# The first self attention's weighing: exponentials as the stationary operand, outputs by tokens

## The reference

```python
qkv = jnp.einsum('bsh,hf->bsf', x, W_qkv)          # 256 tokens x 1536
q8, q_scale = act_quant(q)                          # likewise k8, v8
scores = jnp.einsum('bhqd,bhkd->bhqk', q8, k8) * (q_scale * k_scale) / sqrt(32)
attn = jax.nn.softmax(scores, axis=-1)
out = jnp.einsum('bhqk,bhkd->bhqd', attn, v8) * v_scale
out = out.transpose(0, 2, 1, 3).reshape(B, S, H)
return jnp.einsum('bso,oh->bsh', out, W_out) + b_out   # the caller adds x
```

## Time and profile before

| | us |
|---|---|
| median of 3 runs | 1639.95 (1639.75 to 1640.92) |
| the profiled execution: time | 1641.43 |
| the profiled execution: span | 1639.6 |
| busy in the span: TensorE, its operand loads | 1611.7 (98%), 1250.7 (76%) |
| busy in the span: VectorE, ScalarE, GpSimd | 1086.7 (66%), 690.1 (42%), 131.0 (8%) |

### The profile page before, as it was taken

One profiled execution on the slowest core, in us unless ns is written; L12 is line 12 of the kernel. 1 busy time (PEld: TensorE's weight loads), 2 busy tenths in 40 slices (PEclk: granted clock), 3 DMA queues, 4 the chain that ended last, 5 costly groups with the idle time before them and its releaser, 6 DMA issues.

```text
span 1639.6 us, 22511 instructions
## 1 busy us (share of the span) xinstructions
PE 1611.7 (98%) x8732; PEld 1250.7 (76%) x8732; DVE 1086.7 (66%) x1733; ACT 690.1 (42%) x933; POOL 131.0 (8%) x218
## 2 busy tenths in 40 slices
PE   9999999999999999999999999999999999999998
PEld 7887888888888888888888888887757746555454
DVE  4445777777778778777777779999583741743333
ACT  4334454444445454444454446555331321322221
POOL 0001000000100000010000001111100000011110
PEclk9999999999999999999999999999999999999999
DMA  7876655554565556555454454334320517479994
GB/s 237 226 227 189 161 132 154 149 151 122 170 163 142 148 142 154 119 184 142 119 138 124 128 135 123 102 92 150 121 112 18 205 52 287 197 233 427 422 423 183
DMA packets 125513, 282.93 MB, mean 173 GB/s; under 512 B 7712, under 2 KB 83680, under 8 KB 119264
## 3 DMA queue, kind: packets, MB, share of 16 engines
q1 hardware_dynamic: 103104, 200.75, 38.8%
q0 software_dynamic: 22304, 80.75, 16.5%
HBM read 206.99 MB, written 74.48 MB: 172 GB/s over the span
## 4 chain that ended last, share of the span: by engine, by line
PE 84%; DVE 8%; issue 3%; ACT 3%; DMA 2%; POOL 0%; SPq 0%; DVEq 0%; ACTq 0%
PE bank L478 19%; PE bank L41 19%; PE bank L448 17%; PE bank L500 6%; PE bank L2109 5%; PE bank L1728 3%; PE bank L499 3%; PE bank L2148 2%; PE bank L2134 2%; PE bank L526 1%; DVE e_parts L851 1%; PE bank L2138 1%; DVE S L830 1%; PE bank L2094 1%; DMA v_dram<-v_out 1%
## 5 line engine op out<-in xcount | busy, mean ns | idle before, releaser
L478 PE MATMUL bank<-wv_parts,cT_hi 128*128 128x512 f32 x1024 | 333.8, 390 | 1.7 <-DMA wv_parts<-wv_dram 1.6
L478 PEld LDWEIGHTS bank<-wv_parts,cT_hi 128*128 128x128 f32 x1024 | 192.3, 188 | 42.4 <-DMA wv_parts<-wv_dram 2.0
L851 DVE TENSOR_TENSOR e_parts<-S,e_parts 128x1024 fp32r<-128x1024 f32 (+1 forms) x129 | 156.8, 1215 | 85.5 <-ACT e_parts L656 83.3
L448 PE MATMUL bank<-cT_hi,wk_hi 128*128 128x512 f32 x512 | 204.7, 400 | 0.7 <-DVE cT_lo L783 0.7
L448 PE MATMUL bank<-cT_hi,wk_lo 128*128 128x512 f32 x512 | 199.8, 390 | 0.0
L448 PE MATMUL bank<-cT_lo,wk_hi 128*128 128x512 f32 x512 | 199.7, 390 | 0.0
L647 ACT ACTIVATE S<-S 128x1024 f32<-128x1024 f32 (+1 forms) x129 | 135.8, 1053 | 151.7 <-DVE S L830 151.1
L478 PE MATMUL bank<-wv_parts,cT_lo 128*128 128x512 f32 x512 | 199.3, 389 | 0.0
L843 DVE TENSOR_TENSOR esum<-esum,S 128x512 f32<-128x512 f32 x210 | 144.9, 690 | 71.7 <-ACT S L647 68.1
L656 ACT CAST e_parts<-S 128x1024 fp32r<-128x1024 f32 (+1 forms) x129 | 134.8, 1045 | 135.7 <-PE bank L500 129.5
L803 DVE TENSOR_TENSOR mx<-mx,S 128x512 f32<-128x512 f32 x222 | 152.8, 688 | 13.5 <-ACT S L641 9.6
(11 more groups left out here) (289 smaller groups left out, 2588.4 us busy)
## 6 DMA issues: line engine op xcount, KB each, us to landing
w<-in_w_moe SPq DMA_DIRECT2D x32, 2304.0 KB, 16.6
v_dram<-v_out SPq DMA_DIRECT2D x112, 512.0 KB, 5.0
v_back<-v_dram POOLq DMA_DIRECT2D x110, 512.0 KB
ctx_nat<-in_ctx SPq DMA_DIRECT2D x8, 1024.0 KB, 4.9
ctx_raw<-in_ctxT SPq DMA_DIRECT2D x7, 1024.0 KB, 8.5
v_dram<-v_back SPq DMA_DIRECT2D x14, 512.0 KB, 4.5
v_late<-v_dram POOLq DMA_DIRECT2D x14, 512.0 KB
wv_parts<-wv_dram POOLq DMA_DIRECT2D x6, 1024.0 KB, 8.7
```

Source lines behind the costliest of these rows:

```text
L448: t = e.matmul(banks[b][:], l, r, start=(c == 0 and m == 0), stop=(c == DT - 1 and m == 2))
L478: t = e.matmul(banks[b][:], l, r, start=(c == 0 and m == 0), stop=(c == DT - 1 and m == 2))
L851: e.tensor_tensor(lo, S[:, of_chunk(j, m), :], hi.bitcast(F32), ALU.subtract).then_inc(e_split, 1)
```

## The change

For layer 0 the roles in the weighing are exchanged. The stationary operand is a 128x128 block of exponentials (128 keys by 128 queries of one head); the moving operand is a tile `va` of 33 columns per head, the 32 value columns and a column of ones, which GpSimd fills once. The output has tokens on the partitions, and for each head 32 outputs and their sum. VectorE takes the reciprocal of the sums, 8 numbers per partition for a group, and multiplies into `o`. TensorE transposes `o` (128x128 blocks, one for each token tile), and ScalarE copies the result into `xT`. Group 3 is normalised, turned and copied by token tile. Layer 1 keeps the former way (`weigh_features`, `normalise_features`), with other counts in its waits. The diff, cut to its core:

```diff
@@ memory of the stage
-                (f"{tag}v8", [P, TT, D], F32), (f"{tag}eT", [P, RING, TT * T], F32), (f"{tag}inv", [P, T], F32),
+                (f"{tag}va", [P, TT, SH, SHD + 1], F32), (f"{tag}eT", [P, RING, TT * T], F32), (f"{tag}o", [P, TT, P], F32),
...
+        HC = SHG * (SHD + 1)
+        TILES = (slice(0, TT),), (slice(0, TT),), (slice(0, TT),), (slice(0, 1), slice(1, 2))
+        def values_out(f, i):
+            return W_BANK[:, i * HC:(i + 1) * HC] if f < 3 else banks[4 + i][:, 0:HC]
+        def out_turned(f, tiles):
+            bank = W_BANK if f < 2 else banks[0][:] if f == 2 else (banks[3][:], twin[:, 0:D])[tiles.start]
+            return bank[:, 0:(tiles.stop - tiles.start) * P]
+        def parts_done(k, f, n=0):
+            return 5 * k + f + n + 1
@@ gpsimd_attention
+                e.memset(att_mem[0][10][:, :, :, SHD:], 1.0).then_inc(consts_set, 1)
@@ tensor_attention
+                if f in (1, 2):
+                    e.wait_ge(ao_moved, parts_done(k, f - 1))
+                for i in range(TILES[f][n].start, TILES[f][n].stop):
+                    for r in range(SHG):
+                        h = SHG * f + r
+                        for kt in range(TT):
+                            t = e.matmul(values_out(f, i)[:, r * (SHD + 1):(r + 1) * (SHD + 1)],
+                                         eT[:, h % RING, kt * T + i * P:kt * T + (i + 1) * P], va[:, kt, h, :],
+                                         start=(kt == 0), stop=(kt == TT - 1))
+                t.then_inc(as_weighed, 1)
...
+            def turn_out(f, n=0):
+                tiles = TILES[f][n]
+                e.wait_ge(ao_normed, parts_done(k, f, n))
+                if f == 2:
+                    e.wait_ge(as_max, base + SH)
+                for m, i in enumerate(range(tiles.start, tiles.stop)):
+                    t = e.transpose(out_turned(f, tiles)[:, m * P:(m + 1) * P], o[:, i, :], ident[:])
+                t.then_inc(ao_turned, 1)
...
                 turn_maxima(f)
                 if f < 2 and k == 0:
                     stay_awake(e, W_BANK, 3 - f)
+                if f >= 2 and k == 0:
+                    turn_out(f - 2)
                 if f == 3:
                     project_out(0, 0)
                 scores_turned(f)
...
             project_out(1, 0)
             weigh_group(3)
+            if k == 0:
+                turn_out(2)
+                weigh_group(3, 1)
             project_out(0, 1)
+            if k == 0:
+                turn_out(3, 0)
             project_out(0, 2)
+            if k == 0:
+                turn_out(3, 1)
             project_out(0, 3)
@@ scalar_attention
+            def move_out(f, n=0):
+                tiles = TILES[f][n]
+                e.wait_ge(ao_turned, parts_done(k, f, n))
+                e.copy(xT[:, f, tiles.start * P:tiles.stop * P], out_turned(f, tiles)).then_inc(ao_moved, 1)
...
             for f in range(4):
                 move_maxima(f)
+                if f >= 2 and k == 0:
+                    move_out(f - 2)
                 for r in range(SHG):
                     raise_head(f, r)
+            if k == 0:
+                move_out(2)
+                for n in range(TT):
+                    move_out(3, n)
@@ vector_attention
+                e.wait_ge(as_weighed, parts_done(k, f, n))
+                if f:
+                    e.wait_ge(ao_turned, parts_done(k, f - 1))
+                own.done(e.reciprocal(inv, got[:, :, :, SHD]))
+                own.wait(e)
+                e.scalar_tensor_tensor(o[:, tiles, :].rearrange("p n (r c) -> p n r c", c=SHD), got[:, :, :, 0:SHD],
+                                       sc[:, 5:6] if k == 0 else 1.0, inv.unsqueeze(3).to_broadcast([P, tiles.stop - tiles.start, SHG, SHD]),
+                                       ALU.mult, ALU.mult).then_inc(ao_normed, 1)
```

More of the change, by code:

```diff
@@ L100, in build @@
         own = Steps(vector_step)
-        IDENT_SET, ATT_SET, LOW_ONES, MASKS_SET, SLOTS_COUNTED, SLOTS_SET, IDS_COUNTED, IDS_SET = 4, (8, 9), 10, 12, 15, 17, 18, 19
+        IDENT_SET, ATT_SET, LOW_ONES, MASKS_SET, SLOTS_COUNTED, SLOTS_SET, IDS_COUNTED, IDS_SET = 4, (9, 10), 11, 13, 16, 18, 19, 20
         def gpsimd_constants(e):
@@ L1104, in build @@
             "mag_found mag_max quant_scaled quant_mag quant_val quant_done")
-        as_done, as_max, as_negs, as_turned, as_moved, as_doneT, as_raised, as_summed, as_weighed, ao_moved = sems(
-            "as_done as_max as_negs as_turned as_moved as_doneT as_raised as_summed as_weighed ao_moved")
+        as_done, as_max, as_negs, as_turned, as_moved, as_doneT, as_raised, as_summed, as_weighed, ao_normed, ao_turned, ao_moved = sems(
+            "as_done as_max as_negs as_turned as_moved as_doneT as_raised as_summed as_weighed ao_normed ao_turned ao_moved")
         att_out, att_added = sems("att_out att_added")
@@ L1123, in value_bank, with group_out @@
             return W_BANK[:, 0:T] if f < 3 else banks[4][:, 0:T]
+        HC = SHG * (SHD + 1)
+        TILES = (slice(0, TT),), (slice(0, TT),), (slice(0, TT),), (slice(0, 1), slice(1, 2))
+        def values_out(f, i):
+            return W_BANK[:, i * HC:(i + 1) * HC] if f < 3 else banks[4 + i][:, 0:HC]
+        def group_out(f, tiles):
+            bank = W_BANK[:, 0:TT * HC] if f < 3 else banks[4 + tiles.start][:, 0:HC]
+            return bank.rearrange("p (n r c) -> p n r c", r=SHG, c=SHD + 1)
+        def out_turned(f, tiles):
[3 more added lines that the diff above has]
+            return 5 * k + f + n + 1
         def qk_bank(k, n):
@@ L1184, in tensor_attention @@
         def tensor_attention(e, k):
-            w, w_out, _, _, _, xn, qkT, v, q8, k8, v8, eT, _, _, _, _ = att_mem[k]
-            qs, ks, vs = (q8, k8, v8) if k == 0 else (qkT[:, 0:4, :], qkT[:, 4:8, :], v)
+            w, w_out, _, _, _, xn, qkT, v, q8, k8, va, eT, o, _, _, _ = att_mem[k]
+            qs, ks = (q8, k8) if k == 0 else (qkT[:, 0:4, :], qkT[:, 4:8, :])
             base = SH * k
@@ L1226, in scores_turned, with weigh_group @@
                 t.then_inc(as_doneT, 1)
-            def weigh_group(f):
+            def weigh_group(f, n=0):
                 e.wait_ge(as_raised, base + SHG * (f + 1))
@@ L1235, in weigh_group, with weigh_features @@
                         e.wait_ge(av_moved, TT * (k + 1))
+                if k:
+                    return weigh_features(f)
+                if f in (1, 2):
[8 more added lines that the diff above has]
+                t.then_inc(as_weighed, 1)
+            def weigh_features(f):
                 if f == 1:
-                    e.wait_ge(ao_moved, 4 * k + 1)
+                    e.wait_ge(ao_moved, parts_done(k, 0))
                 if f == 2:
@@ L1245, in weigh_group @@
                 if f == 2:
-                    e.wait_ge(ao_moved, 4 * k + 2)
+                    e.wait_ge(ao_moved, parts_done(k, 1))
                 for kt in range(TT):
@@ L1249, in weigh_group @@
                         h = SHG * f + r
-                        t = e.matmul(value_bank(f)[head_rows(r)], vs[:, kt, h * SHD:(h + 1) * SHD], eT[:, h % RING, kt * T:(kt + 1) * T],
+                        t = e.matmul(value_bank(f)[head_rows(r)], v[:, kt, h * SHD:(h + 1) * SHD], eT[:, h % RING, kt * T:(kt + 1) * T],
                                      start=(kt == 0), stop=(kt == TT - 1))
                 t.then_inc(as_weighed, 1)
+            def turn_out(f, n=0):
[6 more added lines that the diff above has]
+                t.then_inc(ao_turned, 1)
             def project_out(i, c):
-                e.wait_ge(ao_moved, 4 * k + c + 1)
+                e.wait_ge(ao_moved, parts_done(k, c, i if c == DT - 1 and k == 0 else 0))
                 t = e.matmul(OUT_OF[i][:], xT[:, c, i * P:(i + 1) * P], w_out[:, c, :], start=(c == 0), stop=(c == DT - 1))
@@ L1369, in raise_head @@
                     if f >= 2:
-                        e.wait_ge(as_weighed, 4 * k + f - 1)
+                        e.wait_ge(as_weighed, parts_done(k, f - 2))
                 if k == 0 and h == RING - 2:
@@ L1395, in scalar_attention @@
                 move_maxima(f)
+                if f >= 2 and k == 0:
+                    move_out(f - 2)
                 for r in range(SHG):
                     raise_head(f, r)
+            if k == 0:
+                move_out(2)
+                for n in range(TT):
+                    move_out(3, n)
         def vector_attention(e, k):
-            _, _, b_out, _, b_v, xn, qkT, v, q8, k8, v8, _, inv, mx, rest, sc = att_mem[k]
+            _, _, b_out, _, b_v, xn, qkT, v, q8, k8, va, _, o, mx, rest, sc = att_mem[k]
+            by_head = va[:, :, :, 0:SHD]
             tensors = (qkT[:, 0:4, :], qkT[:, 4:8, :], v[:])
@@ L1416, in scales, with round_to_e4m3 @@
                 e.tensor_scalar(sc[:, 22 + n:23 + n], sc[:, 6 + n:7 + n], 2.0 ** 20, None, ALU.mult).then_inc(quant_scaled, 1)
-            def round_to_e4m3(n, o):
+            def round_to_e4m3(n, to):
                 t = tensors[n]
```

(33 more changed lines are left out.)

## The result

| | before | after |
|---|---|---|
| median of the runs, us | 1640.28 (1639.75 to 1640.92) | 1663.41 (1661.13 to 1665.6) |
| ratio | 1 | 1.0139, 95% interval 1.0125 to 1.0153 |
| the profiled execution: time, span | 1641.43, 1639.6 | 1664.06, 1662.3 |
| mean granted TensorE clock of the span | 0.999 | 0.988 |

The account below looks back on a forecast made before the run. TensorE was taken to bound the kernel (84% of the chain), VectorE before 1211.7 us in the stage. Added TensorE time 4 x 1.78 + 0.9 = 8.0 us, less 0.9 idle: 1639.95 + 7.1 = 1647.0 us, range 1645.5 to 1648.5.

Parts of the forecast that it names:

- The price of an instruction: First self attention, TensorE: each 33-column weighing instruction costs 0.114 us, so a group takes 3.65 us against 1.87.
- Rivals 1: Operands change faster in the weighing than in the rows read: 0.08 us per instruction, +2.8 us, 1642.8 us; chance 6%.
- 2: Only moving columns count in the weighing: about 0.03 us per instruction, -1.1 us, 1638.9 us, not slower; chance 3%.
- 4: Operand loads are not drawn ahead of products at all: 0.188 us each, +16.6 us, 1656.6 us; chance 3%.
- The strided write: VectorE's normalising product writes quantised values with a stride: taken as 0, bound 0 to +1.2 us.
- The walk: Step-by-step timeline of the first self attention from 1203.72 us: residual add at 1228.3 instead of 1221.14, +7.1 us.
- weighing 1: Weighing of the second group of four heads on TensorE: starts at 1210.35 us instead of 1209.50, ends at 1214.0.
- weighing 2: Weighing of the third group of four heads on TensorE: starts at 1216.7 us instead of 1213.41, +3.3 us.
- VectorE's saving: Normalising takes 0.7 instead of 2.24 us per group; the 1.5 us go at once into waiting for the first group.
- rival 3: TensorE's clock falls after waits or thin products: one fall +8.9 us, two +10.6, 1648.9 to 1650.6 us; chance 9%.
- granted clock 1.00: Expected sign in the profile after: everything behind the add shifted by the same amount, with TensorE's clock at 1.00.
- Behind the stage: After the first self attention: a later layer normalisation means a later end, the whole shift passed on; second self attention unchanged.

## Why the prediction was wrong, point by point

- **The price of an instruction** was forecast at 0.114 us, between 8 and 128 columns. Measured at full clock: 0.113 in the stage, 0.1125 alone with 132 columns. Right. Rivals 1, 2 and 4 fall with it. The strided write of the quantised values, taken at 0, takes 1.23 us where it took 1.22. One figure beside the sum was off: 1.87 us for 32 instructions are 0.058 us each, not 0.055, which changes nothing in the sum.
- **The walk.** Right to within 0.3 us in every step at full clock, as far as the run with 132 columns can stand for 33: weighing 1 starts 6.80 us after weighing 0 (forecast 6.63), weighing 2 after 13.27 (12.98), the add after 24.73 (24.6). VectorE's saving was given back at once in a wait for the first group, as forecast (1.54 us in that run, 2.14 after the change).
- **The step that failed** is rival 3, "The clock falls", and with it "granted clock 1.00" in the last part. It was given 9% and priced at one or two falls of 3.5 us, on the ground that "TensorE is never idle for a whole microsecond in the walk". The ground is true (the longest wait for an output was 0.61 us) and beside the point. The only fall in the trace of before came behind an idle microsecond, and I took idleness for the cause. After the change TensorE's clock fell while it was busy for 2.00 of 2.00 us, about 3 us into the thin products of group 0 and again 3 us into those of group 2. It stayed down over everything that ran between them, waits and wider products included: about 17 us, then 14. A third fall of 3.4 us came in the feed-forward part; the run with 132 columns has one like it, so it is not tied to the thin products, and its cause stays open.
- **The sum as it came out**, from the two profiled executions: the stage starts 0.33 us later (1204.05 instead of 1203.72); the walk at full clock costs 24.73 - 17.42 = 7.3; the half clock within the stage 38.02 - 24.73 = 13.3; the fall behind it leaves 420.2 instead of 418.5 us from the add to the end, 1.8. Together 22.7, the difference of the spans. The term "clock" is 15.1, and 0 in my sum; 13.3 of it the thin products explain.
- **Behind the stage** the shift is handed on whole, as forecast, and grows by the 1.8 us of that last fall. The second self attention takes 18.04 us from its first weighing to its add in both (1407.61 to 1425.65 before). After the change it starts here:

```profile
1430.26 1.07 PE L1279 MATMUL bank<-l_eT,ones 128*32 128x256 f32 x16
```

  and its add is at 1448.30.
- What I could have read ahead of the run: in the kernel before, the array is kept streaming in many places where TensorE would wait, by products that no one reads (the earlier trace rows shows one such line, L135), and the stretches of products with few columns that I read are about a microsecond long, as the eight with 8 columns in the earlier trace rows. The trace had no row for what 30 of them do to the clock. A bound was missing there: the whole stage at half clock, 1203.7 to 1228.3 twice over, is up to +24.6 us more, and the result lies inside it.

## What to carry to other kernels

When operands are exchanged so that fewer columns stream per operand, cost it twice: once by the instruction (here a new 128x128 block set 0.11 us, whether 33 or 132 columns followed), and once with everything around it at half clock, unless the trace has a stretch of such products as long as the new one. Columns that ride along while the operand changes can be nearly free (0.113 us with 33, 3.8 us for 32 instructions with 132), and here they held the clock: 99 columns more per product, none of them used, took 14 us off the kernel. A busy share of 1.00 on TensorE is no evidence that its clock will hold; read the granted clock by window.

## What the runs showed of the hardware

- TensorE's granted clock can fall while its recorded busy time has no gap (windows from 1206 to 1210 after the change). It came back at 1224, behind a projection of 512 columns and the turned scores, and at 1241, among projections; after the block of 33 columns by itself it came back at 1239, among products of 512 columns. The Trainium skill (TensorE: Matmul & The Clock Gate, The HAM clock gate) says that a monitor sets the clock by how busy TensorE has recently been. If busy is read as the profile's busy share, the trace does not agree: the share is 2.00 of 2.00 us where the clock falls.
- At half clock the load of an operand takes nearly twice as long as well, so thin products are hit in full:

```profile
L1266 PEld LDWEIGHTS bank<-l_va,l_eT x128: 186/333/338, 1204.0 to 1236.6; 128*128 128x128 f32 x128
```

  186 ns is the minimum, at full clock, and 333 the median; the pitch went from 0.113 to 0.214 us. The same page of the Trainium skill (LDWEIGHTS (loading the stationary operand)) prices a load by its columns alone; for 128 columns that makes an estimate of 107 ns. The pitch at full clock is near it, the pitch at half clock is twice it.
- A product of 4-byte operands in the rounded format is one instruction instead of two at the same pitch, 16 in 1.94 us against 32 in 3.8 us.
